# One piece ahead: the order of high and low weight parts in the expert stage of an attention-and-MoE kernel

## The chip, the cores and the metric

The kernel runs on one core of a Trainium2 chip. The metric is the device time of one execution in microseconds (us). Before the change three runs gave 2074.08, 2075.52 and 2075.68 us.

## What is computed

The input is `x`, 4096 tokens of 1024 numbers. A first stage adds to it a product of its normed, fp8-rounded rows with the (also fp8-rounded) context matrix of its batch. The second stage, which fills the time that matters here, adds a mixture of experts:

```python
Xp = x[slots_token].reshape(E, C, d)                 # E = 32 experts, C = 160 slots each
G = jnp.einsum('ecd,edi->eci', Xp, W_gate)           # d = 1024, i = 512
U = jnp.einsum('ecd,edi->eci', Xp, W_up)
Y = jnp.einsum('eci,eid->ecd', jax.nn.silu(G) * U, W_down)
Yf = Y.reshape(EC, d) * slots_w[:, None]
out = jnp.zeros((T, d), x.dtype).at[slots_token].add(Yf)
shared = jax.nn.silu(x @ shared_gate.T) * (x @ shared_up.T) @ shared_down.T
return (out + shared).reshape(b, s, d)
```

A router picks 4 of 32 experts for a token; each expert takes at most 160 tokens. All inputs are float32.

## The kernel before, in words

The float32 products are done in float16 pairs. Every operand is split into a high part, `hi = f16(scale * w)`, and a low part, `lo = f16(scale * w - hi)`, and a product is the sum of three matmuls: hi·hi, hi·lo, lo·hi. ScalarE (ACT) makes the high parts, VectorE (DVE) the low ones.

The kernel first does 16 groups of 256 tokens (attention, router and shared expert), then the 32 experts one after the other. Each engine has its own program; semaphores with names such as `x_lo` count what is done. An expert's weights are 6 pieces of 1 MB: 0 and 1 are W_gate, 2 and 3 W_up, 4 and 5 W_down. Each piece m has one float32 stage in `BIG`, and goes to one of two buffers of `W` (`EW[b]`, b is the parity of the expert). For each piece:

- SP loads it into its stage (`ew_load`, L420), as soon as the low part of the same piece of the expert before is done (`x_lo`). SP goes through the pieces in order.
- ACT makes its high part (`ew_hi`, L802), once it has landed and its buffer is free.
- DVE makes its low part (`ew_lo`, L1218), once the high part is there (`x_hi`).

What each engine does in expert e:

- TensorE (PE): waits until four low parts of the expert (`x_lo >= 6e+4`) and its tokens (`x_xl`) are there, then does four blocks (`ic` = 0 to 3) of gate and up products (L1277) into one of two PSUM banks, each 48 matmuls of 160 columns. Block ic waits until DVE has read the bank of block ic-2 (`x_h`). Then PE transposes the tokens of the next expert (L1418, L1423), waits for `x_lo >= 6e+6` and for the low parts of h of three blocks (`x_hl >= 4e+3`), and does the product `down` (L1456, 24 matmuls of 512 columns, and L1464, 48 short ones for the last 32 slots).
- ACT, in each block: the sigmoid (L833), the high part of h (L837), and in blocks 0 to 2 a high part of a weight piece of the next expert. Then it makes the high part of the next tokens (`et_hi`, L808), more weight pieces, and copies the three results of `down` out of PSUM (`rows_out`, L826).
- DVE, in each block: two products that make h (L1238, L1242), its low part, a subtraction from the high part (L1244), and in blocks 0 to 2 a low part of a weight piece; then the low part of the next tokens (`et_lo`, L1224), and three more weight pieces.
- GpSimd (POOL): gathers the tokens of expert e+2 (L570), scatters the result of expert e and adds it to `out` (L580). A tiny addition (`carry`, L250) stands ahead of each for ordering.

The order of all this within an engine is the order in which the code is written, and each engine goes through it in order. The experts 2 to 29 are in a loop of pairs; 0, 1, 30 and 31 are written out.

Of the kernel before, what the change touches and what calls it, by code (L numbers as in the profile page):

```python
# [46 lines left out]
def moe_kernel(nc, x, ctx_in, mask, router_t, e_bias, w_gate, w_up, w_down, sh_gate, sh_up, sh_down, out,  # L47
               xn_dram, slot_dram):
    T, D = x.shape
    E = router_t.shape[1]  # L50
# [22 lines left out]
    with ExitStack() as stack:  # L73
# [552 lines left out]
        def _(act):  # L626
# [161 lines left out]
            def ew_hi(e, b, m, first=False):  # L788
                act.wait_ge(ld_ew[m], e * 16 + 16)
                if first and m == 0:  # L790
                    act.wait_ge(pe_gu, 8 * GROUPS)
                if not first:

                    wait(act, x_gu if m < 4 else x_dn, e * 4 - 4 if m < 4 else e * 3 - 3)
                stage = ew_stage[m]
                if m < 4:
                    dst = EW[b][m // 2][0][:, (m % 2) * 4:(m % 2) * 4 + 4, :]
                    stage = stage.rearrange("p (k i) -> p k i", k=4)
                else:
                    dst = EW[b][2][0][:, (m % 2) * 2:(m % 2) * 2 + 2, :]  # L800
                    stage = stage.rearrange("p (k i) -> p k i", k=2)
                ac.activation(dst, stage, ACT.Copy, scale=W_SCALE).then_inc(x_hi, 1)  # L802

            def et_hi(e):

                for s in range(3):
                    act.wait_ge(x_xt, e * 3 + (s + 1))
                    ac.activation(et_part(eT[0], s), et_bank(s), ACT.Copy, scale=X_SCALE).then_inc(x_xh, 1)  # L808

            group(GROUPS - 1, 1, front=False, ctx=0,  # L810
                  weights=lambda: [ew_hi(0, 0, m, first=True) for m in range(6)])
            et_hi(0)

            act.wait_ge(pe_dn, 4 * GROUPS)
            for b in range(2):
# [10 lines left out]
                ac.activation(dst, PS[4 + u][:, :] if u < 2 else dn_tail, ACT.Copy,  # L826
                              scale=wts[:, bass.ds(e * 3 + u, 1)]).then_inc(x_y, 1)

            def expert(e, b, more=True):
                for ic in range(KI):  # L830
                    act.wait_ge(x_gu, e * 4 + (ic + 1))
                    wait(act, x_t, e * 4 + (ic - 1 if ic > 1 else 0))
                    ac.activation(sig[ic % 2][:, 0:C], PS[ic % 2][:, 0:C], ACT.Sigmoid, scale=UP_PROJ).then_inc(x_sig, 1)  # L833
                    act.wait_ge(x_h, e * 4 + (ic + 1))
                    if ic == 0:
                        wait(act, x_dn, e * 3)
                    ac.activation(ehT[0][:, ic, :], h32[ic % 2][:, 0:C], ACT.Copy).then_inc(x_hh, 1)  # L837
                    if more and ic < 3:
                        ew_hi(e + 1, 1 - b, ic)
                if more:  # L840
                    et_hi(e + 1)
                    ew_hi(e + 1, 1 - b, 3)
                    ew_hi(e + 1, 1 - b, 4)
                for u in range(3):
                    rows_out(e, b, u)
                if more:
                    ew_hi(e + 1, 1 - b, 5)

            expert(0, 0)
            expert(1, 1)  # L850
            with act.Fori(1, E // 2 - 1) as pair:
                expert(pair * 2, 0)
                expert(pair * 2 + 1, 1)
            expert(E - 2, 0)
            expert(E - 1, 1, more=False)


# [1 line left out]
        def _(dve):  # L859
# [351 lines left out]
            def ew_lo(e, b, m):  # L1211
                dve.wait_ge(x_hi, e * 6 + (m + 1))
                stage = ew_stage[m]
                k = 4 if m < 4 else 2
                src = stage.rearrange("p (k i) -> p k i", k=k)
                cut = (slice(None), slice((m % 2) * k, (m % 2) * k + k), slice(None))
                hi, lo = EW[b][m // 2]
                ve.scalar_tensor_tensor(out=lo[cut], in0=src, scalar=W_SCALE, in1=hi[cut], op0=ALU.mult,  # L1218
                                        op1=ALU.subtract).then_inc(x_lo, 1)
# [10 lines left out]
                      weights=(lambda n: ew_lo(0, 0, n)) if last else None)  # L1230
            et_lo(0)
            ew_lo(0, 0, 4)

            def expert(e, b, more=True):
                for ic in range(KI):
                    bank = PS[ic % 2]
                    dve.wait_ge(x_sig, e * 4 + (ic + 1))
                    ve.scalar_tensor_tensor(out=gup[:, 0:C], in0=bank[:, G:G + C], scalar=H_SCALE * UP_PROJ * UP_PROJ,  # L1238
                                            in1=sig[ic % 2][:, 0:C], op0=ALU.mult, op1=ALU.mult).then_inc(x_t, 1)
                    dve.wait_ge(x_t, e * 4 + (ic + 1))  # L1240
                    wait(dve, x_hh, e * 4 + (ic - 1 if ic > 1 else 0))
                    ve.tensor_tensor(h32[ic % 2][:, 0:C], gup[:, 0:C], bank[:, 0:C], ALU.mult).then_inc(x_h, 1)  # L1242
                    dve.wait_ge(x_hh, e * 4 + (ic + 1))
                    ve.tensor_tensor(ehT[1][:, ic, :], h32[ic % 2][:, 0:C], ehT[0][:, ic, :],  # L1244
                                     ALU.subtract).then_inc(x_hl, 1)

                    if ic == 0:
                        ew_lo(e, b, 5)
                    elif more and ic < 3:
                        ew_lo(e + 1, 1 - b, ic - 1)  # L1250
                if more:
                    et_lo(e + 1)
                    for m in range(2, 5):
                        ew_lo(e + 1, 1 - b, m)

            expert(0, 0)
# [261 lines left out]
```

## Time and profile before

| what | value |
|---|---|
| median of three runs | 2075.52 us (2074.08 to 2075.68) |
| the profiled execution, its time | 2081.25 us |
| its span, as the profile shows it | 2079.6 us |
| mean granted clock of TensorE | 0.99 |
| the expert stage | from about 1353 us to the end |

The profile is of one execution. Starts are in us from the start of the span. "Idle before" is the time in which an engine stood still ahead of an instruction, and `<-` names what ended it. The ends of matmuls are modelled and matmuls overlap.

### The profile page before, as it was taken

Reading aid. Unit: us, or ns where it says so; the run is one execution under the profiler, and the core shown is the slowest. Engines: PE = TensorE matmul, PEld = TensorE weight load, DVE = VectorE, ACT = ScalarE, POOL = GpSimd, SP = SyncE. Lnnn points to the kernel's source line nnn. Section 1 sums busy time; section 2 is a strip of 40 time slices with the busy share of each in tenths; the row PEclk is TensorE's granted clock in tenths of the full one; section 3 lists DMA queues with packets and bytes.
Section 4 is the critical chain, followed back from the end, with each engine's and each line's share of the span. In section 5 each row is a group of like instructions: output and inputs, shape, how many; then the busy total and the mean of one; then the engine's idle time right before and its main releaser. Section 6 shows DMA issues by size and latency. Waiting matters only on the chain.

```text
span 2079.6 us, 45099 instructions
## 1 busy us (share of the span) xinstructions
PE 1875.9 (90%) x17857; PEld 1440.7 (69%) x17872; DVE 1402.0 (67%) x2535; ACT 897.5 (43%) x1269; POOL 560.4 (27%) x613
## 2 busy tenths in 40 slices
PE   0038999999999999999999999999999999999997
PEld 0017578668767767866876786688778778778776
DVE  5787675575567557557644653488888888888884
ACT  8564222222222222212221221367767777777773
POOL 2100111210210111021011111445455445445442
PEclk9988999999999999999999999999999999999999
DMA  9925322212312222231221124299999999999994
GB/s 377 372 55 192 110 67 69 86 58 73 92 61 71 74 83 62 63 100 42 52 82 62 41 62 161 43 380 334 346 334 335 348 333 333 349 329 338 345 340 100
DMA packets 93267, 371.94 MB, mean 179 GB/s; under 512 B 21264, under 2 KB 25392, under 8 KB 68560
## 3 DMA queue, kind: packets, MB, share of 16 engines
q1 hardware_dynamic: 68144, 311.16, 39.8%
q0 software_dynamic: 23808, 58.81, 12.4%
q8 instruction: 91, 1.49, 0.3%
q14 instruction: 40, 0.33, 0.1%
q10 hardware_dynamic: 1184, 0.15, 0.0%
HBM read 314.79 MB, written 55.35 MB: 178 GB/s over the span
## 4 chain that ended last, share of the span: by engine, by line
PE 69%; DVE 14%; issue 6%; ACT 2%; DMA 1%; POOL 0%; SPq 0%; DVEq 0%; ACTq 0%; POOLq 0%
PE ps L1277 45%; PE ps L1288 16%; DVE W L1218 9%; PE ps L1315 5%; PE ps L1342 1%; DVE XT L1224 1%; DVE SG L1242 1%; DVE SG L1238 1%; ACT XT L808 1%; ACT HH L837 1%; PE ps L1360 1%; DMA X<-in_x 1%; PE ps L1298 1%; DVE W L964 1%; ACT SG L833 0%
## 5 line engine op out<-in xcount | busy, mean ns | idle before, releaser
L1277 PE MATMUL ps<-XT,W 128*128 128x256 f16 (+1 forms) x12288 | 1119.6, 253 | 46.3 <-DVE W L1218 39.8
L1277 PEld LDWEIGHTS ps<-XT,W 128*128 128x128 f16 x12288 | 1026.6, 98 | 135.3 <-issue 54.7
L1218 DVE SCALAR_TENSOR_TENSOR W<-BIG,W 128x2048 f16<-128x2048 f32 x192 | 433.6, 2285 | 1.5 <-ACT W L802 1.4
L250 POOL TENSOR_TENSOR expo<-expo 128x1 f32<-128x1 f32 x159 | 160.9, 1012 | 753.3 <-ACT FR L678 296.9
L802 ACT ACTIVATE W<-BIG 128x2048 f16<-128x2048 f32 x192 | 362.6, 1910 | 0.0
L1288 PE MATMUL ps<-W,HH 128*128 128x512 f16 x1536 | 340.9, 380 | 2.0 <-DVE e_pr L1091 2.0
L1288 PEld LDWEIGHTS ps<-W,HH 128*128 128x128 f16 x1536 | 150.6, 98 | 177.8 <-DVE e_pr L1091 2.5
L744 ACT ACTIVATE SG<-ps 128x256 f32<-128x256 f32 x128 | 49.0, 383 | 467.4 <-PE ps L1277 458.7
L1137 DVE SCALAR_TENSOR_TENSOR SG<-ps,SG 128x256 f32<-128x256 f32 x128 | 54.4, 425 | 257.2 <-ACT SG L744 257.2
L1456 PE MATMUL ps<-W,HH 128*128 128x512 f16 x768 | 171.0, 379 | 0.0
L513 POOL TENSOR_TENSOR rs<-ve,expo 128x1 f32<-128x1 f32 x32 | 17.8, 558 | 566.9 <-DVE ve L985 566.9
L520 POOL DMA_INDIRECT slots<-payload,dest x128 | 137.4, 1074 | 43.0 <-issue 43.0
L1118 DVE SCALAR_TENSOR_TENSOR X<-ps,X 128x512 f32<-128x512 f32 x64 | 44.1, 689 | 131.8 <-PE ps L1288 111.9
L1456 PEld LDWEIGHTS ps<-W,HH 128*128 128x128 f16 x768 | 75.1, 98 | 83.4
L1298 PE MATMUL ps<-identb,FR 128*128 128x128 bf16 x256 | 18.5, 227 | 120.9 <-DVE FR L907 116.5
L749 ACT ACTIVATE HH<-SG 128x256 f16<-128x256 f32 x128 | 53.3, 417 | 132.1 <-DVE SG L1142 132.1
L702 ACT ACTIVATE XT<-ps 128x512 f16<-128x512 f32 x64 | 35.1, 594 | 173.3 <-PE ps L1342 114.8
L570 POOL DMA_INDIRECT FR<-xn_rows,gix x64 | 98.4, 1538 | 32.2 <-issue 32.2
L580 POOL DMA_INDIRECT out_rows<-X,six x64 | 102.3, 1598 | 15.1 <-issue 14.6
L1315 PE MATMUL ps<-BIG,FR 128*128 (+1 forms) x465 | 102.8, 379 | 1.0
L1298 PEld LDWEIGHTS ps<-identb,FR 128*128 128x128 bf16 x256 | 16.5, 102 | 121.7 <-issue 113.6
L837 ACT ACTIVATE HH<-SG 128x160 f16<-128x160 f32 x128 | 43.1, 336 | 122.6 <-DVE SG L1242 111.7
(172 smaller groups left out, 1819.4 us busy)
## 6 DMA issues: line engine op xcount, KB each, us to landing
BIG<-in_w_gate SPq DMA_DIRECT2D x64, 1024.0 KB, 7.2
BIG<-in_w_up SPq DMA_DIRECT2D x64, 1024.0 KB
BIG<-in_w_down SPq DMA_DIRECT2D x64, 1024.0 KB, 8.0
X<-in_x SPq DMA_DIRECT2D x16, 1024.0 KB, 5.1
X<-in_mask POOLq DMA_DIRECT2D x16, 1024.0 KB, 8.1
xn_rows<-FR SPq DMA_DIRECT2D x32, 512.0 KB, 2.7
out_rows<-X SPq DMA_DIRECT2D x32, 512.0 KB
W<-in_x SPq DMA_DIRECT2D x6, 2048.0 KB, 19.6
```

The costliest lines, as they stand in the source:

```text
L250: return engine.tensor_tensor(expo[:, col:col + 1], expo[:, 0:1], expo[:, 0:1], ALU.add)
L520: gp.indirect_dma_start(out=slot_dram[:, :], out_offset=bass.IndirectOffsetOnAxis(ap=dest[:, m:m + 1], axis=0), in_=payload[:, m, :], in_o ...
L570: gp.indirect_dma_start(out=dst, out_offset=None, in_=src[:, :], in_offset=bass.IndirectOffsetOnAxis(ap=gix[:, 2 * b + u:2 * b + u + 1], a ...
L580: gp.indirect_dma_start(out=dst[:, :], out_offset=bass.IndirectOffsetOnAxis(ap=six[:, 2 * b + u:2 * b + u + 1], axis=0), in_=src, in_offse ...
L802: ac.activation(dst, stage, ACT.Copy, scale=W_SCALE).then_inc(x_hi, 1)
L837: ac.activation(ehT[0][:, ic, :], h32[ic % 2][:, 0:C], ACT.Copy).then_inc(x_hh, 1)
L1218: ve.scalar_tensor_tensor(out=lo[cut], in0=src, scalar=W_SCALE, in1=hi[cut], op0=ALU.mult, op1=ALU.subtract).then_inc(x_lo, 1)
L1277: ins = te.matmul(out_ps, a[:, k, cols], b[:, k, :], start=n == 0, stop=n == len(steps) - 1)
L1288: ins = te.matmul(out_ps, a[:, k, toks], b[:, k, cols], start=n == 0, stop=n == len(steps) - 1)
L1298: ins = te.transpose(bank[:, k * P:(k + 1) * P], xq[j][:, k * P:(k + 1) * P], identb[:, :])
L1315: ins = te.matmul(PS[2 + h][:, :], xqT[:, k, j * P:(j + 1) * P], BIG[:, bass.ds(ctx_at, HALF)], start=k == 0, stop=k == KD - 1)
L1456: ins = te.matmul(PS[4 + h][:, :], a[:, k, 0:P], w[:, k, h * HALF:(h + 1) * HALF], start=k == 0 and n == 0, stop=k == KI - 1 and n == 2)
```

## The change

Three places in the order change, and nothing in the operations:

1. ACT makes high part 0 of expert 1 ahead of expert 0, and in each expert high part 0 of the expert after the next at the very end, behind high part 5. The blocks 0, 1, 2 hold the pieces 1, 2, 3 (before 0, 1, 2), and only piece 4 stands between `et_hi` and `rows_out` (before 3 and 4).
2. DVE makes low part 5 of expert 0 ahead of expert 0. In the blocks 0, 1, 2 of an expert it makes the pieces 0, 1, 2 of the next expert (before: piece 5 of this expert, then 0 and 1 of the next), and behind `et_lo` the pieces 3, 4, 5 (before 2, 3, 4).
3. On DVE this low part of a piece stands between the second product of h and the subtraction (before: behind the subtraction).

```diff
@@ -810,6 +810,7 @@
             et_hi(0)
+            ew_hi(1, 1, 0)
 
             act.wait_ge(pe_dn, 4 * GROUPS)
@@ -826,7 +827,7 @@
-            def expert(e, b, more=True):
+            def expert(e, b, more=True, ahead=True):
                 for ic in range(KI):
@@ -836,22 +837,23 @@
                     ac.activation(ehT[0][:, ic, :], h32[ic % 2][:, 0:C], ACT.Copy).then_inc(x_hh, 1)
                     if more and ic < 3:
-                        ew_hi(e + 1, 1 - b, ic)
+                        ew_hi(e + 1, 1 - b, ic + 1)
                 if more:
                     et_hi(e + 1)
-                    ew_hi(e + 1, 1 - b, 3)
                     ew_hi(e + 1, 1 - b, 4)
                 for u in range(3):
                     rows_out(e, b, u)
                 if more:
                     ew_hi(e + 1, 1 - b, 5)
+                if more and ahead:
+                    ew_hi(e + 2, b, 0)
...
-            expert(E - 2, 0)
+            expert(E - 2, 0, ahead=False)
@@ -1230,6 +1232,7 @@
             et_lo(0)
             ew_lo(0, 0, 4)
+            ew_lo(0, 0, 5)
@@ -1240,17 +1243,14 @@
                     ve.tensor_tensor(h32[ic % 2][:, 0:C], gup[:, 0:C], bank[:, 0:C], ALU.mult).then_inc(x_h, 1)
+                    if more and ic < 3:
+                        ew_lo(e + 1, 1 - b, ic)
                     dve.wait_ge(x_hh, e * 4 + (ic + 1))
                     ve.tensor_tensor(ehT[1][:, ic, :], h32[ic % 2][:, 0:C], ehT[0][:, ic, :],
                                      ALU.subtract).then_inc(x_hl, 1)
-
-                    if ic == 0:
-                        ew_lo(e, b, 5)
-                    elif more and ic < 3:
-                        ew_lo(e + 1, 1 - b, ic - 1)
                 if more:
                     et_lo(e + 1)
-                    for m in range(2, 5):
+                    for m in range(3, 6):
                         ew_lo(e + 1, 1 - b, m)
```

On DVE, in expert 0 (the part of the program from `et_lo(0)` to the end of block 1), before: W is a low part of a weight piece, SG the two products for h, HH the subtraction, XT the tokens.

```order
L1224 SCALAR_TENSOR_TENSOR XT<-ps,XT 128x8x32 [waits x_xh]
L1218 SCALAR_TENSOR_TENSOR W<-BIG,W 128x2048 [waits x_hi]
L1238 SCALAR_TENSOR_TENSOR SG<-ps,SG 128x160 [waits x_sig]
L1242 TENSOR_TENSOR SG<-SG,ps 128x160 [waits x_t]
L1244 TENSOR_TENSOR HH<-SG,HH 128x160 [waits x_hh]
L1218 SCALAR_TENSOR_TENSOR W<-BIG,W 128x2048 [waits x_hi]
L1238 SCALAR_TENSOR_TENSOR SG<-ps,SG 128x160 [waits x_sig]
```

And of the changed kernel, at the same place:

```order
L1226 SCALAR_TENSOR_TENSOR XT<-ps,XT 128x8x32 [waits x_xh]
L1220 SCALAR_TENSOR_TENSOR W<-BIG,W 128x2048 [waits x_hi] x2
L1241 SCALAR_TENSOR_TENSOR SG<-ps,SG 128x160 [waits x_sig]
L1245 TENSOR_TENSOR SG<-SG,ps 128x160 [waits x_t]
L1220 SCALAR_TENSOR_TENSOR W<-BIG,W 128x2048 [waits x_hi]
L1249 TENSOR_TENSOR HH<-SG,HH 128x160 [waits x_hh]
L1241 SCALAR_TENSOR_TENSOR SG<-ps,SG 128x160 [waits x_sig]
```

The low part of a piece has moved ahead of the subtraction HH, and a second one stands ahead of the first block.

On ACT, from the high part of the tokens in expert 0 to the first high part of a weight piece in expert 1, before: XT is `et_hi`, W a high part of a weight piece, X `rows_out`, SG the sigmoid, HH the high part of h.

```order
L808 ACTIVATE XT<-ps 128x8x32 [waits x_xt]
L802 ACTIVATE W<-BIG 128x2048 [waits ld_ew3]
L802 ACTIVATE W<-BIG 128x2048 [waits ld_ew4]
L826 ACTIVATE X<-ps,wts 128x512 [waits x_dn,consts_ready] x2
L826 ACTIVATE X<-ps,wts 128x256 [waits x_dn,consts_ready]
L802 ACTIVATE W<-BIG 128x2048 [waits ld_ew5]
L833 ACTIVATE SG<-ps 128x160 [waits x_t,x_gu]
L837 ACTIVATE HH<-SG 128x160 [waits x_dn,x_h]
L802 ACTIVATE W<-BIG 128x2048 [waits x_gu,ld_ew0]
```

Of the changed kernel:

```order
L808 ACTIVATE XT<-ps 128x8x32 [waits x_xt]
L802 ACTIVATE W<-BIG 128x2048 [waits ld_ew4]
L827 ACTIVATE X<-ps,wts 128x512 [waits x_dn,consts_ready] x2
L827 ACTIVATE X<-ps,wts 128x256 [waits x_dn,consts_ready]
L802 ACTIVATE W<-BIG 128x2048 [waits ld_ew5]
L802 ACTIVATE W<-BIG 128x2048 [waits x_gu,ld_ew0]
L834 ACTIVATE SG<-ps 128x160 [waits x_t,x_gu]
L838 ACTIVATE HH<-SG 128x160 [waits x_dn,x_h]
L802 ACTIVATE W<-BIG 128x2048 [waits x_gu,ld_ew1]
```

One high part has gone from ahead of `rows_out` to behind it, where it stands ahead of the next sigmoid and waits for stage 0 (`ld_ew0`).

## Rows read from the trace of the kernel before

**Rows 1.** The page, busy us, share of the span, instructions

```profile
PE 1875.9 (90%) x17857; PEld 1440.7 (69%) x17872; DVE 1402.0 (67%) x2535; ACT 897.5 (43%) x1269; POOL 560.4 (27%) x613
```

**Rows 2.** Groups of PE, 1353 to 2060: busy us, mean ns, idle before and releaser

```profile
L1277 PE MATMUL ps<-XT,W 128*128 128x160 f16 x6124 | 429.1, 233 | 39.8 <-DVE W L1218 39.8
```

**Rows 3.** The chain that ended last, one boundary: start, us, what

```profile
1641.59 2.30 DVE W L1218
1643.88 0.22 issue
1644.11 5.91 PE ps L1277 x83
```

**Rows 4.** Timeline of one expert in the loop: start, us, engine, line, operation

```profile
1621.63 13.45 PE L1277 MATMUL ps<-XT,W 128*128 128x160 f16 x192 [1.30 <-DVE W L1218]
...
1625.18 0.30 ACT L833 ACTIVATE SG<-ps 128x160 f32<-128x160 f32 x1 [2.16 <-PE ps L1277]
...
1625.88 0.32 DVE L1242 TENSOR_TENSOR SG<-SG,ps 128x160 f32<-128x160 f32 x1
1626.31 0.34 ACT L837 ACTIVATE HH<-SG 128x160 f16<-128x160 f32 x1 [0.83 <-DVE SG L1242]
1626.56 1.90 ACT L802 ACTIVATE W<-BIG 128x2048 f16<-128x2048 f32 x1
1626.68 0.32 DVE L1244 TENSOR_TENSOR HH<-SG,HH 128x160 f16<-128x160 f32 x1 [0.48 <-ACT HH L837]
...
1626.92 2.28 DVE L1218 SCALAR_TENSOR_TENSOR W<-BIG,W 128x2048 f16<-128x2048 f32 x1
...
1632.43 0.30 ACT L833 ACTIVATE SG<-ps 128x160 f32<-128x160 f32 x1 [0.46 <-PE ps L1277]
...
1633.85 0.33 DVE L1244 TENSOR_TENSOR HH<-SG,HH 128x160 f16<-128x160 f32 x1 [0.40 <-ACT HH L837]
...
1636.01 5.34 PE L1456 MATMUL ps<-W,HH 128*128 128x512 f16 x24
...
1637.51 0.24 POOL L250 TENSOR_TENSOR expo<-expo 128x1 f32<-128x1 f32 x1 [3.85 <-DMA out_rows<-X,six]
...
1638.46 3.72 ACT L802 ACTIVATE W<-BIG 128x2048 f16<-128x2048 f32 x2
1639.39 6.68 DVE L1218 SCALAR_TENSOR_TENSOR W<-BIG,W 128x2048 f16<-128x2048 f32 x3
...
1641.29 1.49 PE L1464 MATMUL ps<-W,HH 128*32 128x256 f16 x48
...
1642.06 1.64 ACT L826 ACTIVATE X<-ps,wts 128x512 f32<-128x512 f32 x3
1643.56 1.94 ACT L802 ACTIVATE W<-BIG 128x2048 f16<-128x2048 f32 x1
1643.92 2.21 POOL L250 TENSOR_TENSOR expo<-expo 128x1 f32<-128x1 f32 x1 [6.06 <-ACT X L826]
...
1644.11 13.45 PE L1277 MATMUL ps<-XT,W 128*128 128x160 f16 x192 [1.33 <-DVE W L1218]
```

**Rows 5.** Timelines of SP and of all engines, the first expert

```profile
1351.16 0.98 SPq L420 DMA_DIRECT2D BIG<-in_w_gate  x2
...
1352.55 4.66 PE L1277 MATMUL ps<-XT,W 128*128 128x160 f16 x65 [1.78 <-DVE XT L1224]
...
1356.15 0.30 ACT L833 ACTIVATE SG<-ps 128x160 f32<-128x160 f32 x1 [4.63 <-issue]
```

**Rows 6.** Transfers from 1600 to 1700; landings of L420 there

```profile
DMA packets 5901, 33.45 MB, mean 335 GB/s; under 512 B 697, under 2 KB 1251, under 8 KB 2523
...
q1 hardware_dynamic: 3809, 27.67, 73.2%
q0 software_dynamic: 2092, 5.78, 23.1%
...
DMA to landing us min/median/max: 7.0/7.7/8.2
```

**Rows 7.** Stretches: busy us (x) by engine, PEclk, DMA share, GB/s

```profile
1599.18:1621.63 22.45, 21.15 (x274) 17.82 (x275) 18.54 (x22) 16.01 (x21) 10.84 (x11) 1.00 0.97 340
1621.63:1644.11 22.48, 21.15 (x275) 17.83 (x275) 18.54 (x22) 16.02 (x21) 11.01 (x11) 1.00 0.96 335
1352.55:1374.69 22.14, 21.14 (x274) 17.80 (x275) 18.35 (x22) 14.33 (x20) 5.82 (x8) 1.00 1.00 399
```

## The prediction

> **What bounds the kernel now.** I read the page first: over the whole span PE is busy 90%, VectorE (DVE) 67% and ScalarE (ACT) 43% [rows 1]. An average over stages says little, so next came the grouped instructions of PE for the 31 experts from 1353 us on: all of PE's idle time there stands before the gate/up product (L1277), 39.8 us, and all of it is ended by DVE's low parts (L1218) [rows 2]. The chain of waits shows the same at one boundary between experts: a low part from 1641.59, 0.22 us of hand-over, and then the product at 1644.11 [rows 3]. The product of expert e needs `x_lo >= 6e+4`, the first four low parts; before, the third and fourth of them are made in the tail of DVE's work for expert e-1, behind `et_lo`. In the timeline of one expert, from 1621.63 to 1644.11, PE's last tail matmul of `down` ends by the profile at 1641.29 + 1.49 = 1642.78, and PE then stands for 1.33 us [rows 4]. So the stage is paced by PE with one wait on DVE at every boundary, 39.8 / 31 = 1.28 us on the mean.
>
> All times below that are called "at +t" count from the start of the product of the expert, S = 1621.63. The period is 22.48 us [rows 4].
>
> **The change, part by part.** No instruction is added or taken away (192 high and 192 low parts before and after); everything is a shift by one piece.
>
> 1. *The gate.* Low parts 0, 1, 2 of the next expert now stand in the blocks 0, 1, 2, and the tail behind `et_lo` holds 3, 4, 5. Before, the tail held 2, 3, 4, and low part 3 was the second of it. Three take 6.68 us from 1639.39 and each lasts 2.28 us [rows 4], so the starts are 2.20 apart: part 3 ended at 1643.87, and as first of the tail it ends at 1641.67, which is 1.1 us ahead of PE's own end at 1642.78. The wait of 1.28 us at each boundary goes. What is late next is PE itself. PE has three waits to pass there, and the hand-over of 0.22 us is the nearest row for their cost [rows 3]; against it, matmuls overlap (192 in 13.45 us are 70 ns apart [rows 4], much less than one lasts), so a row of matmuls without a wait between can start up to 0.2 us before the modelled end of the last. I take 0, with bounds -0.2 and +0.2.
>
> 2. *Low part between h and the subtraction.* In before, DVE waited for ACT's copy of h (L837) and then subtracted: h's product starts at +4.25, the subtraction at +5.05, the low part at +5.29 [rows 4]. Now the low part starts when h is done, at about +4.6 after an undisturbed start, and the subtraction waits 2.28 us for it. Queued behind it are the next block's two products. Per block DVE now needs 2.28 for the low part, 0.33 for the subtraction, and 0.35 + 0.35 for the steps up to the next h, in all 3.3 us; PE delivers a block every 13.45 / 4 = 3.36 us. So the DVE chain keeps pace, just. The one place where PE needs a subtraction early is `x_hl >= 4e+3` (that of block 2) ahead of `down`, which starts at 1636.01 = +14.38. The third sigmoid starts at +10.80, when PE is done [rows 4]; h is done 1.02 later at +11.82 (as 1625.18 to 1625.88 + 0.32), the low part ends at +14.10 and the subtraction at +14.43; with the hand-over of 0.22 the `down` matmuls start at +14.65 where +14.38 was possible. That is a new stall of up to 0.27 us, and 0.1 if the waits in PE's queue are passed sooner. I take 0.2 per expert, from 1 to 29 or 30. Before, this subtraction had nearly 2 us to spare.
>
> 3. *High part 0 of the expert after next, put behind `rows_out` and high part 5.* ACT's idle time is ample over all, but this one stands in front of the next sigmoid. Before, high part 5 starts at 1643.56, 0.78 after PE's tail end; this was because ACT came to `rows_out` late (1642.06) behind high parts 3 and 4. Now only one high part stands there, and the third copy follows PE's end at once: high part 5 starts some 0.4 behind it, at +21.55, the second at +23.4, and it ends at +25.2 (two take 3.72 [rows 4]). With a new period of some 21.35 that is +3.9 of the next expert, where the sigmoid could start at +3.55. So it is 0.35 late (bounds: 0.2 and 0.7). The cover: PE reads h of block 0 only ahead of block 2, at 2 x 3.36 = +6.7, and h is done by +3.9 + 1.02 = +4.9; and ACT's own loop (0.24 for the copy, 1.80 for a high part, 1.1 from sigmoid to h, together 3.2) is shorter than 3.36, so that the third sigmoid is on time again. Cost nothing; if the cover were gone every us beyond +4.2 would be a us at step 2.
>
> 4. *The loads.* A stage is loaded again when its low part is done, and the order on SP stays. Now stage 0 is free at about +7.2 and is wanted at +23.4, 16 us later; the others keep between 13 and 19 us. A load lands 7.0 to 8.2 us after its issue [rows 6]. Hidden, with 6 us or more to spare. What it costs if the transfers are the limit is a rival below. POOL: its 2.2 us carry (L250) ahead of a scatter now falls beside low part 5 and not beside part 4, about 1 us later in an expert; it had waited 3.9 us for the scatter before anyway [rows 4].
>
> 5. *The first expert.* ACT now makes high part 0 of expert 1 ahead of the first sigmoid. Its stage is loaded by a DMA issued at 1351.16, and the sigmoid was at 1356.15 [rows 5]. The landing lies between the bare transfer of 1 MB at 399 GB/s [rows 7], 2.6 us, and the 8.2 us of a busy queue [rows 6]; I take the middle, 5.5, as an estimate. The high part then runs from about 1356.8 to 1358.7, and the sigmoid is 2.6 us late (5.3 by the longest landing). PE then waits ahead of block 2 (h at 1359.9, wanted at 1352.55 + 6.7 = 1359.25): 0.9 with the hand-over. The lag of DVE stays, and the subtraction of block 2 is done near 1368.85, where `down` wanted it at 1367.8: 1.3 more. The first boundary therefore gives 1.28 and pays 2.2: a net loss of about 1.0 us, bounds 0 and 3.
>
> The sum, over 31 boundaries: 30 x (1.28 - 0 - 0.2) = 32.4 us saved, 1.0 lost, so 31.4 net. The profiled execution took 2081.25 us by its clock, 1.65 more than its span of 2079.6, and lies 5.7 above the median of the three runs, 2075.52; the change is put on the median: 2075.5 - 31.4 = 2044.1. On the profiled one it would be a span of about 2048. Its own bounds: without step 2 and with the overlap, 30 x 1.48 = 44 saved, 2031; with hand-over, a stall of 0.35, and 3 lost at the start, 30 x 0.73 - 3 = 19 saved, 2057.
>
> **Transfers against the new pace.** From 1600 to 1700 the queues took 73.2% and 23.1% of the 16 DMA engines, 96.3% together, and moved 33.45 MB [rows 6]: 7.51 MB and 21.6 us of engine time per expert of 22.48. At 21.4 us per expert they must give 352 GB/s in place of 335, with packets that take less time. That they can is seen in the first expert: 399 GB/s over 22.14 us, though mostly of weight loads, while 340 and 335 were asked later [rows 7].
> The Trainium skill, page "DMA: Bandwidth & Descriptors", section "Where 436 GB/s comes from", says that for transfers between HBM and SBUF the HBM side binds, at about 358 GB/s per core. By that rule 7.51 MB cost at least 21.0 us, only 0.4 under my period; the row of 399 GB/s disagrees with it for this core alone on its chip, and the measurement decides. The page itself gives 425 GB/s for one core with 16 MB.
>
> **The rivals.**
> *A. The transfers become the bound.* For: 96.3% busy now, and scatters move far less than loads per engine time (5.78 MB in 23.1%, against 27.67 MB in 73.2% [rows 6]). Against: rows 7, and the spare 6 us per stage, which would absorb a deficit of 0.2 us per expert over all 30. If 21.6 us and half of the 0.8 us that the engines are idle now cannot be undercut, the period is 22.0: 30 x 0.45 - 1 = 12.5 saved, 2063; after the spare time, 2057. I give it 2050 to 2066. Chance 0.17.
> *B. Nothing comes of it:* a wait of the same length takes the place of the one removed, the subtraction of block 2 being late by a full 1.3 us. This needs the third sigmoid at +11.9 in place of +10.80, or h's chain at 3.7 us per block. The chain's rows say 3.3, so 0.04; 2071 to 2080.
> *C. Slower:* high part 0 in front of the first sigmoid. It decides where it ends 1.4 us later than I have it, past +5.3, for then step 2 takes back more than 1.28. It would do so if its load landed more than 17.5 us after the issue; the longest is 8.2 now, but a saturated queue lets it grow. With 0.5 us over the break-even, 30 x 0.5 + 1 = 16 us slower, 2091. Chance 0.06.
> *D. More than forecast*, below 2031: it needs the period to fall under 21.0, which PE's own work (22.48 - 1.33 = 21.15) forbids but for the overlap. 0.03.
> *Forecast*: 0.70, itself 2031 to 2057.
>
> **How the numbers follow.** A measurement of this kernel can tell some 0.2%, 4 us, from no change. Faster: forecast, A and D, 0.90. Same: most of B, 0.04. Slower: C, 0.06. The range is that of the forecast, reaching up over most of A: 2031 to 2062, which leaves out B, C, D and the upper end of A, about 0.17. The most likely time is 2044.
>
> **What the next profile would show.** PE's idle time ahead of the product, ended by low parts, falls from 39.8 us to a few; the period of an expert is 21.2 to 21.5; DVE, 18.5 us busy per expert [rows 7], rises to 18.5 / 21.4 = 87% in the stage; PE idles up to 0.3 us ahead of `down` (L1456), ended by the subtraction of h; the first sigmoid of each expert follows a high part without idle time on ACT; DMA gives 350 GB/s or more, and landings lengthen but stay under 13 us. The first expert is longer than 22.14 by about 1 us. Wrong would be: ACT idle ahead of a high part (A or C: the load is late), or PE idle by 1 us ahead of `down` (B).

## The result and the profile after

The changed kernel takes **2037.94 us**, median of 5 runs (2037.16 to 2039.4), against 2074.54 for the kernel before beside it (5 runs, 2073.79 to 2075.68). The ratio is **0.9824 [0.9811, 0.9838]**: 36.6 us are saved where 31.4 were forecast (2044). All medians are of executions in the usual, fast state; one of run 1 was slow, 4095.31 us, and is left out. The profiled execution took 2037.94 us, its span is 2036.3. The profiled execution of before took 2081.25 us and reached the first expert's product 6.5 us later than this one (1352.55 against 1346.09); that stretch holds nothing of the change, so I compare the expert stage by its own starts.

Two lines of the page of the changed kernel follow: the busy time of each engine [rows 1 are those of before], and the shares of the chain of waits that ended last (in before PE had 69% of that chain and DVE 14%):

```profile
PE 1870.2 (92%) x17857; PEld 1439.3 (71%) x17872; DVE 1395.4 (69%) x2535; ACT 896.9 (44%) x1269; POOL 587.8 (29%) x613
...
PE 88%; DVE 2%; DMA 1%; issue 1%; SPq 0%; POOL 0%; ACT 0%; POOLq 0%; ACTq 0%
```

The busy times hardly moved (nothing was added or removed); the span became shorter. The grouped instructions from 1353 to 2060 us say where (busy us, mean ns, then idle before them):

```profile
L1277 PE MATMUL ps<-XT,W 128*128 128x160 f16 x6048 | 424.1, 233 | 3.0 <-DVE SG L1245 3.0
...
L1456 PE MATMUL ps<-W,HH 128*128 128x512 f16 x768 | 171.0, 379 | 1.2 <-DVE HH L1249 1.2
```

The 39.8 us that PE stood before the gate/up product, ended by low parts [rows 2], are gone. The 3.0 and 1.2 us that are left lie all in the first expert. At a boundary between two experts the chain of waits (start, us, what) now holds PE alone, where [rows 3] had a low part and a hand-over in it:

```profile
1618.32 5.18 PE ps L1456 x24
1623.50 1.42 PE ps L1464 x48
1624.92 13.39 PE ps L1277 x192
```

The timeline of one expert, to be laid beside [rows 4] (start, us, engine, line, tiles, count, idle time before it and what ended it). Its product starts at S = 1624.86:

```profile
1624.86 13.46 PE L1277 MATMUL ps<-XT,W 128*128 128x160 f16 x192
...
1627.37 2.29 DVE L1220 SCALAR_TENSOR_TENSOR W<-BIG,W 128x2048 f16<-128x2048 f32 x1 [1.94 <-ACT W L802]
...
1629.04 0.29 ACT L834 ACTIVATE SG<-ps 128x160 f32<-128x160 f32 x1
...
1629.93 0.32 DVE L1245 TENSOR_TENSOR SG<-SG,ps 128x160 f32<-128x160 f32 x1
1630.17 2.28 DVE L1220 SCALAR_TENSOR_TENSOR W<-BIG,W 128x2048 f16<-128x2048 f32 x1
...
1633.24 2.28 DVE L1220 SCALAR_TENSOR_TENSOR W<-BIG,W 128x2048 f16<-128x2048 f32 x1
...
1635.40 0.28 ACT L834 ACTIVATE SG<-ps 128x160 f32<-128x160 f32 x1
...
1636.32 2.28 DVE L1220 SCALAR_TENSOR_TENSOR W<-BIG,W 128x2048 f16<-128x2048 f32 x1
...
1638.52 0.32 DVE L1249 TENSOR_TENSOR HH<-SG,HH 128x160 f16<-128x160 f32 x1
...
1639.24 5.34 PE L1456 MATMUL ps<-W,HH 128*128 128x512 f16 x24
```

To be seen: the product at 1624.86 has no idle time before it; the low parts of the blocks start 3.07 and 3.08 us apart; the subtraction of block 2 (L1249) ends at 1638.52 + 0.32 = 1638.84, and `down` (L1456) starts without a wait at S + 14.38, the very place that it had in before. Two windows show the first expert and this one (columns: window, length, busy PE, PEld, DVE, ACT, POOL, granted clock, DMA share, GB/s):

```profile
1346.09:1371.88 25.79, 21.58 (x275) 17.72 (x275) 19.51 (x22) 14.14 (x18) 4.65 (x7) 1.00 1.00 400
1624.86:1645.94 21.08, 21.08 (x278) 17.81 (x275) 18.44 (x22) 15.95 (x20) 12.21 (x10) 1.00 1.02 360
```

PE is busy for the whole of the second. The same view over 30 periods, from the start of expert 1's product to that of the last expert's, in the kernel before and in the changed one:

```profile
1374.69:2047.86 673.17, 634.41 (x8221) 534.54 (x8221) 555.76 (x631) 479.61 (x601) 324.88 (x296) 1.00 0.96 335
```

```profile
1371.88:2004.33 632.45, 632.45 (x8225) 534.51 (x8221) 550.43 (x631) 478.84 (x600) 355.70 (x295) 1.00 1.00 355
```

That is 673.17 / 30 = 22.44 and 632.45 / 30 = 21.08 us for an expert, and PE's busy time fills the second. So 673.17 - 632.45 = 40.7 us are gained, 1.36 for an expert, and the first boundary, 25.79 us long in place of 22.14, gives 3.65 back. From the last start to the end it is 31.97 us, 0.2 more than before. Together 36.8 us are gained from the first start on; the medians differ by 36.6.

### The profile page after: what moved, and what is told of

It reads as the page before. It is cut to its first block, busy times and chain, and to the rows that moved or that the text cites. A ratio compares the mean times of both kernels' runs of the same rounds, so it can differ in the third digit from the quotient of the medians.

```text
span 2036.3 us, 45113 instructions
## 1 busy us (share of the span) xinstructions
PE 1870.2 (92%) x17857; PEld 1439.3 (71%) x17872; DVE 1395.4 (69%) x2535; ACT 896.9 (44%) x1269; POOL 587.8 (29%) x613
## 4 chain that ended last, share of the span: by engine, by line
PE 88%; DVE 2%; DMA 1%; issue 1%; SPq 0%; POOL 0%; ACT 0%; POOLq 0%; ACTq 0%
PE ps L1277 52%; PE ps L1288 16%; PE ps L1456 8%; PE ps L1315 5%; PE ps L1464 2%; PE ps L1342 1%; PE ps L1418 1%; PE ps L1360 1%; DMA X<-in_x 1%; DMA BIG<-in_w_up 1%; PE ps L1298 1%; DVE W L966 1%; PE ps L1423 0%; PE ps L1366 0%; POOL out_rows L580 0%
## 5 line engine op out<-in xcount | busy, mean ns | idle before, releaser
L250 POOL TENSOR_TENSOR expo<-expo 128x1 f32<-128x1 f32 x159 | 83.1, 523 | 669.7 <-ACT FR L678 294.8
L570 POOL DMA_INDIRECT FR<-xn_rows,gix x64 | 165.6, 2587 | 31.6 <-issue 31.6
L1456 PE MATMUL ps<-W,HH 128*128 128x512 f16 x768 | 171.0, 379 | 1.2 <-DVE HH L1249 1.2
L580 POOL DMA_INDIRECT out_rows<-X,six x64 | 135.7, 2121 | 28.4 <-issue 28.4
L1456 PEld LDWEIGHTS ps<-W,HH 128*128 128x128 f16 x768 | 75.0, 98 | 84.8 <-DVE W L1220 1.4
L695 ACT ACTIVATE FR<-X,nb,rs 128x1024 f32<-128x1024 f32 x32 | 38.1, 1234 | 125.0 <-DVE nb L991 125.0
```

Of the source, the lines that this page charges most:

```text
L250: return engine.tensor_tensor(expo[:, col:col + 1], expo[:, 0:1], expo[:, 0:1], ALU.add)
L570: gp.indirect_dma_start(out=dst, out_offset=None, in_=src[:, :], in_offset=bass.IndirectOffsetOnAxis(ap=gix[:, 2 * b + u:2 * b + u + 1], a ...
L580: gp.indirect_dma_start(out=dst[:, :], out_offset=bass.IndirectOffsetOnAxis(ap=six[:, 2 * b + u:2 * b + u + 1], axis=0), in_=src, in_offse ...
L1456: ins = te.matmul(PS[4 + h][:, :], a[:, k, 0:P], w[:, k, h * HALF:(h + 1) * HALF], start=k == 0 and n == 0, stop=k == KI - 1 and n == 2)
```

## The experiments

The first four runs share one chip, the next four a second and the last three a third. The table has medians, ratios to the kernel before on the same chip, and the period, which is the time from the start of one expert's product to that of the next; "first" is that from expert 0 to expert 1:

| run | us | ratio | period of an expert, us |
|---|---|---|---|
| first expert in the old order | 2036.42 | 0.9821 | 21.08, first 23.29 |
| changed, subtraction ahead of the low part | 2038.72 | 0.9834 | 21.08, first 24.88 |
| low parts one ahead, high parts not | 2228.44 | 1.0749 | 27.3 |
| kernel before, only PE's wait split | 2034.14 | 0.9821 | 21.08, first too |
| changed, short products | 2037.08 | 0.9826 | 20.8 to 20.9, every fifth 22.4 to 22.6 |
| split wait, short products | 2009.15 | 0.9692 | 20.3 |
| before, short products | 2067.01 | 0.9957 | 21.2 to 23.3 |
| changed again | 2038.39 | 0.9831 | 21.08, first 25.44 |
| changed, short products, high part 5 earlier | 2016.14 | 0.9698 | 19.7 to 19.8, every second or third 21.4 to 21.6 |
| split wait again | 2036.46 | 0.9797 | 21.08, first too |
| changed a third time | 2039.40 | 0.9807 | 21.08, first 23.7 |

**1. The first expert as before.** Expert 0 alone keeps the old order of high and low parts (only its low part 5 stays ahead of it); from expert 1 on all is as in the change. The cut shows ACT's side; DVE's goes back in the same way.

```diff
             et_hi(0)
-            ew_hi(1, 1, 0)
...
-                        ew_hi(e + 1, 1 - b, ic + 1)
+                        ew_hi(e + 1, 1 - b, ic if start else ic + 1)
...
-            expert(0, 0)
+            expert(0, 0, start=True)
```

> The changed kernel, but expert 0 in the old order (no high part ahead of its first sigmoid, the low parts behind the subtraction, four low parts in its tail). Theory (the gate is all there is, and the changed kernel loses 3.65 us at the first boundary because ACT waits for a load): the first boundary goes back from 25.79 to 22.1 us, the other 30 stay at 21.08, so 3.7 us less than the changed kernel: 2034.3. Rival (the late start is absorbed later anyway, the loss lies in the first load's way): no change, 2038.

2036.42 us, 0.9821 [0.9809, 0.9834]. The first boundary is 23.29 us. It is 2.5 shorter than in the profile of the changed kernel and 1.6 shorter than in run 2 on the same chip, whose median is 2.3 higher, and the times of the two do not overlap. So the early high part has a price. The boundary did not come back to 22.1. The gate's wait is there again, as in before, but with 2.15 us where it was 1.01 at this boundary. ACT waits for the first load in the old order too, 1.26 us, and the second sigmoid starts 8.28 us after the product where it was 6.84. A part of the loss thus hangs on how late that load lands, wherever its high part stands:

```profile
1353.89 1.91 ACT L802 ACTIVATE W<-BIG 128x2048 f16<-128x2048 f32 x1 [1.26 <-DMA BIG<-in_w_gate]
...
1370.70 1.49 PE L1280 MATMUL ps<-XT,W 128*128 128x160 f16 x19 [2.15 <-DVE W L1221]
```

**2. The subtraction first.** The changed kernel, with the low part moved behind the subtraction in each block.

```diff
-                    if more and ic < 3:
-                        ew_lo(e + 1, 1 - b, ic)
                     dve.wait_ge(x_hh, e * 4 + (ic + 1))
                     ve.tensor_tensor(ehT[1][:, ic, :], h32[ic % 2][:, 0:C], ehT[0][:, ic, :],
                                      ALU.subtract).then_inc(x_hl, 1)
+                    if more and ic < 3:
+                        ew_lo(e + 1, 1 - b, ic)
```

> The changed kernel with the subtraction of h ahead of the low part again, as before the change; pieces one ahead as in the changed kernel. Theory (only the gate counts): low part 3 still ends about 1 us ahead of PE's end, so 2038, within 1 us. Rival (the place of the low part counts, since the DVE chain per block goes from 3.07 back to 3.52 us, over PE's 3.32, and 0.2 us per block add up): PE waits 0.3 to 0.8 us per expert ahead of its last blocks or of the next product, 2047 to 2062.

2038.72 us, 0.9834 [0.9821, 0.9846], and the period is the same 21.08. DVE's timeline shows what the order costs all the same:

```profile
1635.08 0.33 DVE L1247 TENSOR_TENSOR HH<-SG,HH 128x160 f16<-128x160 f32 x1 [0.40 <-ACT HH L838]
1635.32 2.28 DVE L1220 SCALAR_TENSOR_TENSOR W<-BIG,W 128x2048 f16<-128x2048 f32 x1
...
1638.84 2.28 DVE L1220 SCALAR_TENSOR_TENSOR W<-BIG,W 128x2048 f16<-128x2048 f32 x1
```

A block takes 1638.84 - 1635.32 = 3.52 us instead of 3.07: DVE waits 0.40 for ACT's copy of h in each, a wait which the change's order covers with the low part. At PE's pace neither matters. The place of the subtraction is worth nothing here.

**3. The low parts ahead, the high parts not.** ACT keeps the old order; DVE makes low parts 0, 1, 2 of the next expert in blocks 0, 1, 2, behind the subtraction as in run 2. The cut shows ACT's side against the changed kernel.

```diff
-                        ew_hi(e + 1, 1 - b, ic + 1)
+                        ew_hi(e + 1, 1 - b, ic)
                 if more:
                     et_hi(e + 1)
+                    ew_hi(e + 1, 1 - b, 3)
                     ew_hi(e + 1, 1 - b, 4)
```

> Only DVE's order of pieces is changed (one ahead, subtraction first); ACT keeps the order of before, so the high part of a piece is made in the same block as its low part. Theory (ACT has to be one ahead too): each block of DVE waits for the high part, 0.35 + 0.35 + 0.34 + 1.9 + 2.28 = 5.0 us or more per block in place of PE's 3.36; h of block 2 comes near +15.3 where down wants its subtraction at +14.4, low part 3 ends near +24.8, the period is some 25 us: 2074.5 + 31 x 2.5 = 2150. Rival (ACT has slack, its shift is not needed): 2038.

2228.44 us, 1.0749 [1.073, 1.0768], 27.3 us per expert: slower than I expected, 25 (2150 us). The granted clock is 0.95 on the mean from 1380 to 2000 us, which adds a part that I did not separate. DVE's wait for high parts from 1353 to 2020 us (total, times, longest) and its timeline:

```profile
DVE W L1218 <- ACT W L802: 149.0, 123, 2.4
```

```profile
1599.53 2.29 DVE L1218 SCALAR_TENSOR_TENSOR W<-BIG,W 128x2048 f16<-128x2048 f32 x1 [1.47 <-ACT W L802]
...
1604.61 2.29 DVE L1218 SCALAR_TENSOR_TENSOR W<-BIG,W 128x2048 f16<-128x2048 f32 x1 [1.48 <-ACT W L802]
```

Each low part waits 1.47 us for the high part that ACT makes in the same block, and a block takes 1604.61 - 1599.53 = 5.08 us. The two shifts belong together: once DVE works one piece ahead, ACT must too.

**4. Only PE's wait split.** The kernel before, with no piece moved on ACT or DVE. PE waits for the gate's two low parts before the gate product and for the up product's before that one.

```diff
             def expert(e, b, more=True):
-                pe.wait_ge(x_lo, e * 6 + 4)
+                pe.wait_ge(x_lo, e * 6 + 2)
...
                     product(PS[ic % 2][:, 0:C], EW[b][0], eT, KD, cols)
+                    if ic == 0:
+                        pe.wait_ge(x_lo, e * 6 + 4)
                     product(PS[ic % 2][:, G:G + C], EW[b][1], eT, KD, cols).then_inc(x_gu, 1)
```

> The kernel before with nothing moved on ACT or DVE; only PE's wait is split: two low parts (W_gate) ahead of the gate product, the other two ahead of the up product of block 0, 24 matmuls or 1.66 us later. Theory (the gate alone made the 1.28 us, and transfers, ACT and DVE can all keep a period of 21.08): low part 3 is ready 22.24 after the old start, the up product is reached at 21.08 + 1.66 = 22.74, so no wait is left and all 31 boundaries gain 1.36: 2074.5 - 42 = 2032.5. Rival (the pieces had to be one ahead for DVE and ACT to keep up): the wait comes back elsewhere, 2045 to 2074.

2034.14 us, 0.9821 [0.9807, 0.9835]. The timeline (the second line is the third sigmoid of that expert) and PE's group from 1353 to 2060 us:

```profile
1620.93 13.45 PE L1277 MATMUL ps<-XT,W 128*128 128x160 f16 x192
...
1631.10 0.30 ACT L833 ACTIVATE SG<-ps 128x160 f32<-128x160 f32 x1
...
1642.02 3.15 PE L1277 MATMUL ps<-XT,W 128*128 128x160 f16 x43
```

```profile
L1277 PE MATMUL ps<-XT,W 128*128 128x160 f16 x6054 | 424.5, 233 | 0.1
```

The period is 1642.02 - 1620.93 = 21.09, and 0.1 us of idle time is left in the whole stage. The whole gain of the change can be had by moving one wait half a block later, and the first expert isn't made longer.

**5 to 7. Short products.** To see what comes next behind PE, each of three kernels leaves out one of the three matmul passes of the experts' gate and up products (high weights times low tokens), so that PE has about 4 us less to do per expert (17.07 busy in a window of run 7, 21.15 in before's [rows 4]): the changed kernel, the one with the split wait, and the kernel before.

```diff
                 steps = [(a, b, k) for k in range(chunks) for a, b in ((whi, xhi), (whi, xlo), (wlo, xhi))]
+                if short:
+                    steps = [step for n, step in enumerate(steps) if n % 3 != 1]
```

> The changed kernel with one of the three matmul passes (high weights by low tokens) left out of the gate and up products of the experts: PE's own work per expert falls from 21.08 to some 16.65 us, so the next bound shows itself. Theory (DVE is next: 3 blocks of 3.07 us, block 3, et_lo and three low parts): period about 19.6 us, time 2038 - 31 x 1.5 = 1992, and ACT never waits for a load. Rival (the transfers are right behind, as 96% busy engines before the change said): period 20.9 or more, ACT idle ahead of high parts and ended by DMA, 2030 or more.

2037.08 us, 0.9826 [0.9808, 0.9844]. Cutting a fifth of PE's work gave the changed kernel next to nothing, where I had expected 1992: it has a loop of its own, a ring of waits in which each expert's start depends on the one before, and this takes 20.8 to 20.9 us where the clock is full. Some steps of one turn in the chain of waits:

```profile
1604.40 1.88 ACT W L802
...
1617.91 5.35 PE ps L1458 x24
```

The turn is `down`, the third copy of its result, high part 5, low part 5, the three blocks with a low part each, the subtraction of block 2, `down` again. No wait on a transfer is in it, so the rival's reason, the transfers, is not what holds it. The waits from 1380 to 1980 us have DVE's, for high part 5, and PE's, for the subtraction:

```profile
DVE W L1220 <- ACT W L802: 57.8, 28, 3.5
PE ps L1458 <- DVE HH L1249: 57.2, 28, 2.3
```

In the longer periods the granted clock is lower; two windows next to each other (columns as above):

```profile
1454.71:1477.14 22.43, 18.86 (x214) 13.72 (x211) 19.11 (x22) 15.95 (x20) 12.02 (x10) 0.92 1.02 366
1477.14:1498.03 20.89, 17.18 (x215) 13.30 (x211) 17.58 (x21) 15.98 (x20) 11.60 (x10) 1.00 1.00 345
```

> The kernel before with the split gate, and the same pass left out. Theory (DVE's blocks are 3.52 us here since it waits for ACT's copy of h, 0.45 more each): period about 21.0 us, so hardly under 2034, and some 40 us slower than the changed order with the same pass left out: the change's order is worth something only where PE is not the bound. Rival (the orders are alike, or the transfers bind): equal to the changed kernel with the pass left out within 10 us.

2009.15 us, 0.9692 [0.9674, 0.9709]: 28 us faster than the changed kernel with the same work, where I had expected it slower. Its period is 20.3 us, and PE waits for a low part at each of 29 boundaries. Of the 28 us, some 16 are the period at full clock (30 x 0.55); the rest is the first boundary (25.6 us in run 5, 20.8 here) and the longer periods of run 5 at a lower clock. Where PE is not the bound, the order of the change is thus worse than the old one with its wait split. The waits from 1380 to 1980 us, and the transfers from 1600 to 1700:

```profile
PE ps L1279 <- DVE W L1218: 49.8, 29, 1.9
```

```profile
DMA packets 6632, 37.36 MB, mean 374 GB/s; under 512 B 792, under 2 KB 1432, under 8 KB 2872
```

> The kernel before with the same pass left out, whole gate. Theory (in the kernel before DVE's chain and not PE set the pace, and the wait at the boundary was PE waiting for it): PE's 4.4 us per expert are hardly felt, the period goes from 22.45 to 21.0 to 22.2, time 2030 to 2066. Rival (PE sets the pace and the wait of 1.28 us is a fixed cost on top): the period falls by nearly 4.4 us, 1940.

2067.01 us, 0.9957 [0.9938, 0.9976] (6 runs, 2057 to 2071.5), 1 us over what I had expected at most. Some 130 us less work for PE (32 x 4.08, at full clock) save only 6 to 9 us (by the medians and by the ratio). Two experts next to each other, the first sigmoid of each, and the waits from 1380 to 1980 us:

```profile
1637.50:1658.71 21.21, 17.07 (x211) 13.33 (x211) 18.52 (x22) 15.78 (x21) 9.77 (x11) 1.00 1.02 358
1658.71:1680.88 22.17, 18.54 (x211) 14.99 (x211) 18.45 (x22) 15.79 (x21) 10.94 (x11) 0.91 0.99 343
```

```profile
1639.92 0.30 ACT L833 ACTIVATE SG<-ps 128x160 f32<-128x160 f32 x1 [1.03 <-PE ps L1279]
...
1662.08 0.30 ACT L833 ACTIVATE SG<-ps 128x160 f32<-128x160 f32 x1 [1.98 <-PE ps L1279]
```

```profile
PE ps L1279 <- DVE W L1218: 83.9, 27, 3.3
```

What PE is spared it spends for the most part in waiting for low parts (3.1 us each time). The pace is that of a loop: PE's first block, DVE's four blocks, the low part of the tokens, the two low parts behind it, and the next product. Of PE's speed this loop feels the first block alone. At full clock the first sigmoid is at 1639.92 - 1637.50 = +2.42 instead of the +3.55 of before, 1.13 us sooner, and the period is 21.21 in place of 22.44, 1.23 shorter. In the next period, with a lower clock, the sigmoid is at +3.37, 0.95 later, and the period is 0.96 longer. Was it the same loop in the kernel before? Its chain of waits goes through the first 144 matmuls to the third sigmoid (at 1632.43, for 0.30), but DVE is busy with a low part just as long, until 1630.44 + 2.29 = 1632.73:

```profile
1621.63 10.78 PE ps L1277 x144
```

```profile
1630.44 2.29 DVE L1218 SCALAR_TENSOR_TENSOR W<-BIG,W 128x2048 f16<-128x2048 f32 x1
```

So there the way through three blocks of PE and the way through one block of PE and DVE's blocks were equally long, and run 7, with PE shorter, shows the second.

**8. The changed kernel again**, on the second chip.

> The changed kernel once more, on the chip of these runs: 0.982 of the kernel before, 2036 to 2039. It serves to set the split gate and the first expert's order against the same kernel.

2038.39 us, 0.9831 [0.9818, 0.9845]; starts 25.44 us apart at the first boundary and 21.08 at all others.

**9. High part 5 earlier.** The changed kernel with short products (the same pass left out), and high part 5 ahead of the third copy of `down`'s result.

```diff
+                    if more and u == 2:
+                        ew_hi(e + 1, 1 - b, 5)
                     rows_out(e, b, u)
-                if more:
-                    ew_hi(e + 1, 1 - b, 5)
```

> The changed kernel with the short products (one of three matmul passes of gate and up left out), and high part 5 moved on ACT from behind the third copy of rows_out to ahead of it. Theory (the changed order has a loop of its own of 20.8 us: end of down, third copy, high part 5, low part 5, first h product, three blocks, subtraction of block 2, down): without the link from the third copy to high part 5 the first h product starts 0.9 us earlier after the product's start and the period falls to about 19.9 us where the granted clock is full, 1995 to 2015. Rival (the transfers hold it at 20.8): no change against the same kernel with high part 5 behind, 2037.

2016.14 us, 0.9698 [0.968, 0.9715], 1 us over the upper end that I had expected. With the link from the third copy to high part 5 taken out, the period at full clock falls from 20.8 to 19.8 or 19.7 us. So that link was in the loop. DVE's wait on ACT ahead of low parts (1380 to 1980 us) falls from 57.8 us in run 5 to 36.1:

```profile
DVE W L1220 <- ACT W L802: 36.1, 29, 2.3
```

**10 and 11. The split wait and the changed kernel side by side** on the third chip.

> The split gate once more, on one chip with the changed kernel: all 31 boundaries seamless and no late start, 4.4 us less than the changed kernel: 2034. If the two are equal within 1 us, the saving at the start is lost elsewhere.

> The changed kernel on the same chip as the split gate: 2038, 4.4 us more than the split gate.

2036.46 us, 0.9797 [0.9784, 0.9811], and 2039.40 us, 0.9807 [0.9793, 0.982]. The split wait is 2.9 us faster here, where I had expected 4.4, and 4.2 by runs 4 and 8 on different chips. In the profiles of these two runs the first boundary is 21.07 us with the split wait and 23.7 with the change (product at 1349.92, the next at 1373.65), which makes 2.7 of the 2.9 us. The first boundary of the changed kernel is not the same in each execution: 25.79, 25.44 and 23.7 us in its three profiles. The intervals of the two ratios overlap, so 3 to 4 us is the direction and rough size, no more.

## Why the prediction was right, and where it was not

**Step 1, the gate.** Right. The wait of 1.28 us went, and PE was next. I had taken the seamless start at 0 with bounds of 0.2 either side; the period fell by 1.36, so the overlap is worth 0.08. Run 4 shows that this step is the whole gain: the same 21.08 us without any of the other steps.

**Step 2, the stall ahead of `down`.** This is the step that failed: the forecast held 0.2 us for each of 30 experts, 6 us in all, and the stall does not exist. The mis-sized term is the end of the subtraction of block 2, put at +14.43 and measured at 1638.84 - 1624.86 = +13.98, while `down` needs it ahead of +14.38. Of these 0.45 us, 0.26 are the third sigmoid: the forecast took it over from before at +10.80, and it is at 1635.40 - 1624.86 = +10.54. That alone would have left next to no stall (14.43 - 0.26 + 0.22 = 14.39). The other 0.19 are overlap on DVE: from the sigmoid to the low part it takes 0.92 us and not 1.02, and from there to the end of the subtraction 2.52 and not 2.61. The low part starts 0.24 us after the start of the product of 0.32 us before it (1629.93 to 1630.17). By the same overlap a block of DVE takes 3.07 us and not 3.3, so DVE gains on PE's 3.36 (the forecast's figure) from block to block. In part this is luck: DVE entered block 0 with a wait of 1.94 us for high part 5 which I had not named. I had only ACT's side of that delay. Run 5 measures how near it was: the loop through high part 5 takes 20.8 to 20.9 us, 0.2 to 0.3 us under PE's 21.08. Run 2 shows that it isn't the place of the subtraction that decides.

**Step 3, high part 0 ahead of the sigmoid.** Right: the first sigmoid is at 1629.04, +4.18 (forecast +3.9, bound 0.7 late), and it cost nothing. Even in the loop of run 5 it is high part 5 that stands in the chain, not this one.

**Step 4, the loads.** Right. From 1600 to 1700 the landings of the weight loads and, from another view, the transfers of the changed kernel are:

```profile
DMA to landing us min/median/max: 6.0/8.3/9.6
...
DMA packets 6311, 35.64 MB, mean 356 GB/s; under 512 B 757, under 2 KB 1361, under 8 KB 2712
```

I had asked for 350 GB/s or more and landings under 13 us. After the first expert ACT never waits for a weight load. Rival A, the transfers as the bound at 22.0 us, is refuted twice: by the period of 21.08, and by run 6, where 374 GB/s are moved at 20.3 us per expert. The Trainium skill, page "DMA: Bandwidth & Descriptors", section "Where 436 GB/s comes from", puts the limit of one core's traffic with HBM at about 358 GB/s. The changed kernel at 356 looks just like that limit, but run 6 goes beyond it with 374. So for this core, which works alone on its chip, the traces do not agree with it as a bound; the 425 GB/s that the prediction quotes from the same page had left that open.

**Step 5, the first expert.** Right in kind and too small in size: 3.65 us lost in the profiled execution where 1.0 was forecast, outside the bound of 3. (Against the same 22.14 us, the profiles of runs 2, 8 and 11 lose 2.7, 3.3 and 1.6 us.) The first expert in the timelines of SP, ACT and PE [rows 5 are those of before]:

```profile
1344.70 1.29 SPq L420 DMA_DIRECT2D BIG<-in_w_gate  x2
```

```profile
1352.70 1.91 ACT L802 ACTIVATE W<-BIG 128x2048 f16<-128x2048 f32 x1 [7.64 <-DMA BIG<-in_w_gate]
1354.52 0.29 ACT L834 ACTIVATE SG<-ps 128x160 f32<-128x160 f32 x1
```

```profile
1346.09 6.80 PE L1277 MATMUL ps<-XT,W 128*128 128x160 f16 x96 [1.77 <-DVE XT L1226]
1355.57 3.49 PE L1277 MATMUL ps<-XT,W 128*128 128x160 f16 x48 [2.68 <-DVE SG L1245]
1359.38 3.49 PE L1277 MATMUL ps<-XT,W 128*128 128x160 f16 x48 [0.31 <-DVE SG L1245]
...
1365.18 5.34 PE L1456 MATMUL ps<-W,HH 128*128 128x512 f16 x24 [1.22 <-DVE HH L1249]
```

The load was issued at 1344.70, and ACT could go on at 1352.70: 8.0 us, not the 5.5 of the middle between a bare transfer and a busy queue. The sigmoid is at +8.43 in place of +3.60, 4.8 us late, and PE waits 2.68 + 0.31 + 1.22 = 4.21 us in three places where I had 2.2 in two. I should have taken the busy value: it was the first of six loads issued within 6 us. In run 11 the same load went out at 1348.53 and ACT could go on at 1355.41, 6.9 us, and the boundary was 2 us shorter; what makes the landing vary is open.

The sum then was 31.4 and is 36.6: 2.4 us more from step 1, 6 more from step 2, 2.65 less from step 5; that makes 5.8 more, and 5.2 were measured.

**"Paced by PE with one wait on DVE"** was the wrong picture of the kernel before, though it gave the right number. The wait that returned at every boundary belonged to a loop through PE's first block or first three, DVE's blocks and two low parts; with PE 4.1 us shorter, run 7 has that loop at 21.21 us, and the wait grows to 3.1. The change broke it, and PE's own 21.08 us appeared, because the next loop (run 5) was just shorter. Rivals B, C and D did not come: no wait took the old one's place, and high part 0 waited for its load only at the very start.

**Open.** In before, the third sigmoid stands at +10.80, and its row has a wait of 0.46 us for PE [rows 4]; in the changed kernel it stands at +10.54 and does not wait. PE's rows are the same in both. The order on ACT and DVE is not the reason: run 4 has the old order, and there it stands at 1631.10 - 1620.93 = +10.17. I found no row that explains it. Also open is by how much the split wait is ahead in general, 2.9 or 4.2 us.

## What to carry to other kernels

Before work is moved between engines to make a wait shorter, look at what the waiting instruction really reads: here a wait for four pieces stood ahead of a product that reads two, and splitting it gave all of the gain, with nothing to pay at the start (2034.14 and 2036.46 us on two chips, against 2038 to 2039 for the change). When a wait is gone, shorten the engine that has become the bound, by leaving out work, and see what the period does: here it showed the next loop and its margin (0.2 to 0.3 us), and that the change is 28 us behind the split wait once PE is not the bound (runs 5 and 6). PE's idle time in the profile of the changed kernel, zero from expert 1 on, told nothing of either. A piece made "one ahead" at the start of a stage has nothing to hide its load behind; price that at the landing time of a busy queue (6.9 to 8.0 us here).

## What the hardware showed that was not expected

With short products PE idles for some 3 to 4 us per expert, and in runs 5, 7 and 9 the granted clock, 1.00 in the windows of the full kernels, is 0.92 or 0.91 over some periods: for a part of these PE had 1.2 instead of 2.4 GHz. In the pairs shown such a period is 1.0 us (22.17 against 21.21 in run 7) and 1.5 us (22.43 against 20.89 in run 5) longer than its neighbour. In run 9 it is every second or third one; two neighbours there (columns as above):

```profile
1740.34:1761.70 21.36, 18.68 (x214) 13.71 (x210) 19.19 (x22) 15.77 (x21) 15.83 (x11) 0.92 1.03 388
1761.70:1781.52 19.82, 17.02 (x215) 13.30 (x211) 17.70 (x21) 15.91 (x21) 13.43 (x10) 1.00 0.99 344
```

PE's busy time is 18.68 against 17.02 us for the same work. In the kernel before, whose PE paused 1.3 us per expert, the clock stayed at 1.00 [rows 7]. It stayed at 1.00 in run 6 too, from 1380 to 1980 us, though PE was busy for only 507.37 of these 600 us, 3.1 us idle per expert; in the full-clock period of run 9 above it is idle for 2.8 of 19.82 us. So the idle time per expert alone does not decide it. What brings it about, no run here tells. The short products measure the other loops a little too long where it occurs, and I read those loops from the periods at full clock.
